# Attended values on 16 tiles of the TensorE array, turned by VectorE out of PSUM

## The reference, cut to what matters

```
attn = jax.nn.softmax(jnp.einsum('bthd,bshd->bhts', q, k) * scale, axis=-1)
attn_out = jnp.einsum('bhts,bshd->bthd', attn, v).reshape(Bc, Tc, INNER)
attn_out = attn_out @ out_w + out_b
x = x + gate1 * attn_out
```

## Time and profile before

| | |
|---|---|
| time, median of 3 runs | 338.66 us (338.62 to 338.73) |
| span of the profiled execution, first to last instruction | 336.9 us |
| busy: PE, DVE, ACT, POOL | 330.3, 215.2, 183.1, 121.5 us |
| chain that ended last | PE 88%, DVE 6%, ACT 4% |

### The profile page before, as it was taken

One profiled execution on the slowest core, in us unless ns is written; L12 is line 12 of the kernel. 1 busy time (PEld: TensorE's weight loads), 2 busy tenths in 40 slices (PEclk: granted clock), 3 DMA queues, 4 the chain that ended last, 5 costly groups with the idle time before them and its releaser, 6 DMA issues.

```text
span 336.9 us, 9816 instructions
## 1 busy us (share of the span) xinstructions
PE 330.3 (98%) x4197; PEld 299.6 (89%) x4197; DVE 215.2 (64%) x420; ACT 183.1 (54%) x356; POOL 121.5 (36%) x107
## 2 busy tenths in 40 slices
PE   8999999999999999999999999999999999999986
PEld 8989989899998989899898999889998889998765
DVE  3846966815858953505167236679565789886896
ACT  3754654454426365356423816478535576628794
POOL 1373405000934762555311413032620123304591
PEclk9999999999999999999999999999999999999999
DMA  7984930500045540110010000100010200200011
GB/s 241 369 283 175 299 129 2 151 8 2 2 146 170 158 158 34 64 33 2 3 56 11 2 20 14 43 24 2 2 62 2 64 3 2 64 2 2 0 33 62
DMA packets 20834, 24.41 MB, mean 72 GB/s; under 512 B 1780, under 2 KB 18328, under 8 KB 20792
## 3 DMA queue, kind: packets, MB, share of 16 engines
q1 hardware_dynamic: 20416, 23.50, 21.5%
q10 hardware_dynamic: 376, 0.30, 0.3%
HBM read 22.68 MB, written 1.11 MB: 71 GB/s over the span
## 4 chain that ended last, share of the span: by engine, by line
PE 88%; DVE 6%; ACT 4%; issue 1%; POOL 0%; DVEq 0%; ACTq 0%
PE proj_banks L564 40%; PE out_bank L564 15%; PE att_banks L657 8%; PE wide_banks L564 4%; PE turn_bank L564 3%; PE proj_banks L627 3%; PE wide_banks L848 2%; PE att_banks L564 2%; PE att_banks L892 1%; PE wide_banks L657 1%; ACT work L1855 1%; PE att_banks L848 1%; PE wide_banks L731 1%; ACT L1714 1%; DVE hamax L1466 1%
## 5 line engine op out<-in xcount | busy, mean ns | idle before, releaser
L1721 ACT ACTIVATE q_t<-proj_banks,bias_cols 128x256 f32<-128x256 f32 x64 | 30.6, 477 | 54.3 <-PE proj_banks L564 54.3
L564 PE MATMUL proj_banks<-x_hi,w_hi 128*128 128x256 f32 x252 | 52.8, 291 | 0.0
L564 PE MATMUL proj_banks<-x_lo,w_hi 128*128 128x256 f32 x252 | 50.7, 283 | 0.0
L564 PE MATMUL proj_banks<-x_hi,w_lo 128*128 128x256 f32 x252 | 50.7, 283 | 0.0
L1233 DVE TENSOR_TENSOR v_sb<-proj_banks,bv_row 128x512 f32<-128x512 f32 x32 | 21.7, 685 | 32.3 <-PE wide_banks L657 30.6
L564 PEld LDWEIGHTS proj_banks<-x_hi,w_hi 128*128 128x128 f32 x252 | 39.6, 191 | 1.5 <-issue 0.4
L564 PEld LDWEIGHTS proj_banks<-x_hi,w_lo 128*128 128x128 f32 x252 | 39.2, 191 | 0.0
L564 PEld LDWEIGHTS proj_banks<-x_lo,w_hi 128*128 128x128 f32 x252 | 39.2, 191 | 0.0
L657 PEld LDWEIGHTS att_banks<-probs_t,v_sb 32*128 32x128 f32 x512 | 29.8, 186 | 5.5 <-issue 5.4
L657 PE MATMUL att_banks<-probs_t,v_sb 32*128 32x32 f32 x512 | 31.6, 272 | 0.0
L1721 ACT ACTIVATE k_t<-proj_banks,bias_cols 128x256 f32<-128x256 f32 x64 | 30.2, 471 | 0.0
(11 more groups left out here) (324 smaller groups left out, 776.6 us busy)
## 6 DMA issues: line engine op xcount, KB each, us to landing
stage<-in_L_cond_qkv_w SPq DMA_DIRECT2D x16, 256.0 KB, 4.5
gate<-gate_rows_scratch SPq DMA_DIRECT2D x48, 64.0 KB, 2.4
stage<-in_L_cond_qkv_w SPq DMA_DIRECT2D x4, 512.0 KB, 5.0
stage<-in_L_cond_out_w SPq DMA_DIRECT2D x4, 512.0 KB, 4.3
work<-in_L_ffn_w SPq DMA_DIRECT2D x2, 1024.0 KB, 10.0
xin<-in_x SPq DMA_DIRECT2D x7, 256.0 KB, 2.9
bv_row<-in_L_cond_qkv_b SPq DMA_DIRECT2D x4, 256.0 KB, 5.7
work<-in_L_cond_ada_w SPq DMA_DIRECT2D x1, 1024.0 KB, 9.7
```

The lines of the kernel that those rows point to most:

```text
L564: mm = pe.matmul(dst, l, r, start=start and i == 0, stop=stop and i == len(seq) - 1)
L1721: act.activation(dst[:, h, :], proj_bank[h % 2][:, s * QT:(s + 1) * QT], ACT.Identity, bias=bias_cols[:, c:c + 1]).then_inc(qk_kept, 1)
```

## The change

In `attend` the operands change sides: the stationary operand is the 32x32 block of probabilities, the moving one the 32x128 block of values. The result is 32 tokens by 128 features, at the partitions of head h; with the sequence j as row tile and the head h as column tile all 16 tiles of 32x32 are used. A new `at_turn` on VectorE transposes the 32x32 blocks from PSUM into a new `at_raw` (in the memory of `at_lo`), two instructions of 128x512 elements per unit. `at_high` and `at_low` read `at_raw` in SBUF instead of PSUM, and work by tile t instead of by pair of banks. In the turned layout partition h*32+e holds feature d*32+e of head h, so the rows of the output weights are loaded in that order: four transfers for each group instead of one (128 KB each instead of 512 KB). PSUM is free again once `at_turned` is reached, so the waits for `at_lo_made` that guarded the banks become waits for `at_turned`. `out_proj` waits for its own t only, and for `at_lo` in both.

`attend(u - 1)` moves ahead: in units 1 to 7 before the last `qk_unit`, in the first units of the pairs from 8 on before the third, in the second units of the pairs before `v_unit(u, 0)`. In the second units of the pairs up to unit 13 `out_proj(u - 1, 0)` moves behind `ffn1` and the first `hq_turn`, and on VectorE `at_low` moves behind `softmax_shift`.

```diff
-    wo_d = out_w.rearrange("(h p) c -> p h c", p=P)
+    wo_d = out_w.rearrange("(g h d e) c -> g h e d c", g=NG, h=HG, d=HG)
...
+        at_raw = at("at_raw", [P, 2, HG, P], F32, floor.where["at_lo"])
...
         def att_from(u, p):
-            return att_pairs(u)[p][:, :, 0:2 * HG * TB].rearrange("p j (a c) -> p j a c", c=TB)
-
-        def att_to(split, p):
-            return split[:, :, :, 2 * p * TB:2 * (p + 1) * TB].rearrange("p t h (j c) -> p j (t h) c", j=2)
+            return att_pairs(u)[p][:, :, 0:2 * P].rearrange("p j (a c) -> p j a c", c=TB)
+
+        def att_to(p):
+            return at_raw[:, :, :, 2 * p * TB:2 * (p + 1) * TB].rearrange("p t d (j c) -> p j (t d) c", j=2)
...
             def load_wo(g):
-                sp.dma_start(wo_stage, wo_d[:, g * HG:(g + 1) * HG, :]).then_inc(wo_in, 16)
+                for h in range(HG):
+                    sp.dma_start(wo_stage[h * TB:(h + 1) * TB, :, :], wo_d[g, h]).then_inc(wo_in, 16)
...
                 if u > 0:
-                    pe.wait_ge(at_lo_made, 2 * u)
+                    pe.wait_ge(at_turned, 2 * u)
...
-                            dst = att_pairs(u)[j // 2][:, j % 2, (t * HG + h) * TB:(t * HG + h + 1) * TB]
-                            mm = pe.matmul(dst, v_sb[r, t, h * P:(h + 1) * P], probs_t[r, t * HG + h, :],
+                            dst = att_pairs(u)[j // 2][h * TB:(h + 1) * TB, j % 2, t * P:(t + 1) * P]
+                            mm = pe.matmul(dst, probs_t[r, t * HG + h, :], v_sb[r, t, h * P:(h + 1) * P],
                                            start=True, stop=True)
...
-                pe.wait_ge(at_hi_made, 2 * u + 2)
+                pe.wait_ge(at_hi_made, 2 * u + t + 1)
...
-                           late=("lhsT", (at_lo_made, 2 * u + 2)) if t == 0 else None).then_inc(out_mm, 1)
+                           late=("lhsT", (at_lo_made, 2 * u + t + 1))).then_inc(out_mm, 1)
...
-            def at_low(u, p):
-                dve.wait_ge(at_hi_made, 2 * u + p + 1)
-                dve.tensor_tensor(att_to(at_lo, p), att_from(u, p), att_to(at_hi, p).bitcast(F32),
-                                  ALU.subtract).then_inc(at_lo_made, 1)
+            def at_turn(u, p):
+                dve.wait_ge(attended, 2 * u + 2)
+                dve.transpose(att_to(p), att_from(u, p)).then_inc(at_turned, 1)
+
+            def at_low(u, t):
+                dve.wait_ge(at_hi_made, 2 * u + t + 1)
+                dve.tensor_tensor(at_lo[:, t], at_raw[:, t], at_hi[:, t].bitcast(F32), ALU.subtract).then_inc(at_lo_made, 1)
 
             def attention_tail(u):
                 if u > 0:
+                    for p in range(2):
+                        at_turn(u - 1, p)
                     keep_v(u, 0)
...
-            def at_high(u, p):
-                act.wait_ge(attended, 2 * u + 2)
-                act.copy(att_to(at_hi, p), att_from(u, p)).then_inc(at_hi_made, 1)
+            def at_high(u, t):
+                act.wait_ge(at_turned, 2 * u + 2)
+                act.copy(at_hi[:, t], at_raw[:, t]).then_inc(at_hi_made, 1)
```

73 lines of the change are left out of this document (43 added, 30 removed).

## The result

The changed kernel takes 344.17 us (median of 4, 342.68 to 345.94); the kernel before took 338.70 beside it. The ratio is 1.0165, interval 1.0131 to 1.0199. It is slower by 1.65%, where 0.4% faster was forecast (337.3, range 334.2 to 341.2). The profiled execution has a span of 342.7 us. The executions of the changed kernel spread by 1%, those of the kernel before by 0.1%.

A forecast was written before the change was run, and what follows sets the result against it. TensorE, busy 98% of the span, was taken to bound the kernel. Terms summed to a gain of 2.0, less 0.6 for `at_low` waits, about 1.4: span 336.9 to 335.5, with 1.8 around it 337.3 us, range 334.2 to 341.2.

The forecast's parts named there:

- The product: Attend on TensorE, each unit: 0.95 us instead of 1.92, saving 0.97 per unit, 15.5 us if nothing else waited.
- rivals 2 and 3: Middle attend: 1.38 us, 340.7, chance 0.12; attend not shorter, 1.8 to 1.9 us, column tiles taking turns: 344, chance 0.10.
- The turns: Two transposes on VectorE per unit, 0.71 us each: 1.34 with a little overlap, 21.5 us in all.
- less 0.6: Waits of `at_low` beside GpSimd: 0.6 us lost; bounds 0, and 2 us for each of two places on the path.
- The four transfers: Three more weight transfers per group: cost nothing while they land a unit early, their bytes being the same.
- Units 2, 4, 6: `score` or attend starts later behind VectorE's `x1_make`, `tern_keep`, `tern_make`, turns and `keep_v`: 0.6, 1.1 and 0.4 us lost.
- theory 2: Not in the prediction, tested after it: VectorE's instructions with two SBUF inputs wait for GpSimd's.
- Units 3, 5, 7, 8: Time gained: 0.7 us each in units 3, 5 and 7; 0.97 in unit 8, where VectorE is not behind.
- Unit 9: `at_low` comes behind the softmax's shift, `out_proj(8, 0)` waits 0.8 us for `at_lo`: only 0.14 gained.
- Units 12 to 15: VectorE's chain from `probs_t` nearly without a gap: 0.05 us gained in 12 and 13, 0.4 in 14 and 15.
- The tail: After unit 15, turns, `at_high` and `at_low` make `hidden_max` start 1.8 us later; with slack of 0.2, 1.6 lost.
- The rival on this side: Slower by VectorE: turns cost 0.89 us instead of 0.71, or `at_low` waits 2 in two places; 339 to 341, chance 0.18.

The follow-up runs named there:

- pieces: The changed kernel with GpSimd's subtractions on the weights each cut into four of a quarter of the size, nothing left out: 346.23 us, ratio 1.0225.
- one_wo: The changed kernel with one 512 KB transfer of output weights per group again, the order of the weights' rows left out: 343.34 us, ratio 1.0126.
- pool_after: The changed kernel with GpSimd's subtractions for the low parts of the weights replaced by fills with zero: 338.03 us, ratio 0.9986.

## Why the prediction was wrong, point by point

The forecast was 337.3, the time 344.17. Of the 6.9 us between them 4.1 are what `at_low` waited beside GpSimd beyond the 0.6 of the sum, up to 1.9 the four transfers, and about 1 the units 12 to 15.

- **The product.** 0.95 forecast, 0.99 measured, and on average a start every 12.6 ns. Right; so rivals 2 and 3 are out. That the time came to rival 3's 344 is chance: its mechanism isn't there. The Trainium skill's 25 ns between starts ("TensorE: Matmul & The Clock Gate", section "Wait — 56ns, not 53.3ns?") holds no more for 32x32 tiles with 128 columns than for `score`.
- **The turns.** 1.34 per unit forecast; 0.71 and 0.67 measured, less their overlap 1.31. Right.
- **`at_low` beside GpSimd, "less 0.6".** This is the step that failed: the term was 0.6, with 2 us for each of two places, 4 in all, as its upper bound, and it measured 4.7 (units 6 and 9 of pieces), or 6.1 with all that GpSimd's subtractions hold up. The three long `at_low` took 2.46 and 2.86 us in unit 8 and 2.88 in unit 5, and none took over 0.69 with GpSimd's reads gone. The row was there, 2266 ns at L1252, but "once" and "one case in 16" were misread from a minimum, a median and a maximum: four of these 16 took over 1 us in the kernel before, and their mean is 708 ns against a median of 426. I spread the wait as a chance over 32 instructions, when the trace of before shows which of them run beside one of GpSimd's subtractions of 128x1024: both `at_low(7)` beside `w_lo` (138.71 and 139.32, shown above), both `at_low(4)`, at 93.13 and 93.74, beside `f_lo`, and one of unit 8 at the end of a `wo_lo`. Three of these five are the long ones. The Trainium skill has the rule ("SBUF — State Buffer", section "SBUF: two separate sides"): the two engines shut each other out for a whole instruction. The trace agrees, with the 2.46 to 2.88 above. That the changed kernel without GpSimd's reads takes 338.03, near the 337.3 of the forecast, proves less than it seems: unit 2 also gains 1.84 there by weights that come earlier, and four of its ten executions have a stretch at clock 0.50.
- **The four transfers, "nothing while they land a unit early".** This failed too, as a term put at nothing. They are in time themselves; what stands behind them on SyncE is not. It is 0.5 us in unit 1 and 1.4 in unit 2 by one_wo's trace; the medians differ by 0.8. The sum asked only when these transfers land. It left out their issue, 1.4 us for the next transfer, and what they do to the landing of the weights behind them, 7.8 us instead of 5.8 (6.4 in one_wo).
- **Units 2, 4, 6.** In 2 and 4 the sign and the mechanism were right: score(2) waits 1.72 for `keep_v` behind the turns, attend(3) 0.69 for `tern_keep`. In pool_after, where theory 2 is absent, the pitches against before are +0.81, +1.59 and -0.33, forecast +0.6, +1.1 and +0.4 (here plus is time lost). So unit 6 gains without theory 2, and its loss was right in sign by luck: the 1.39 came from GpSimd.
- **Units 3, 5, 7, 8.** +0.7, +0.7, +0.7, +0.97 forecast; 0.72, 0.84, 0.43, 0.94 measured. Right, but for 0.3 in unit 7.
- **Unit 9.** +0.14 forecast, 1.96 lost; the wait of `out_proj(8, 0)` that I worked out as 0.8 is 0.44, and it stands behind score(9), so it counts in the next pitch. In pool_after the unit gains 0.96. The loss comes from unit 8.
- **Units 10, 11.** +0.97 and +0.1 forecast, 0.35 and 0.76 measured: the sum is right, the places are not.
- **Units 12 to 15.** +0.45 forecast, 0.8 lost, of which 0.4 (unit 12) is gone in pool_after. Here VectorE is late, and attend(12) and attend(14), now ahead of `v_unit`, wait 1.04 each for `probs_t`. The releaser isn't named, but the end of the transpose is at 228.31, and attend(12) starts at 228.41 (VectorE, then TensorE):

```profile
227.86 0.45 DVE L1263 STREAM_TRANSPOSE probs_t<-scores 128x256 f32<-128x256 f32 x1
```

```profile
228.41 0.30 PE L660 MATMUL att_banks<-v_sb,probs_t 32*32 32x128 f32 x2 [1.04 <-issue]
```

- **The tail.** 1.6 forecast, 61.2 - 59.6 = 1.6 measured. Right, and where it was said to be. VectorE in order of time, of the kernel before, to be held together with the earlier trace rows:

```profile
283.75 1.21 DVE L1463 TENSOR_TENSOR h_odd<-h_odd,g_row 128x1024 f32<-128x1024 f32 x1
...
286.30 1.21 DVE L1466 TENSOR_REDUCE hamax<-h_odd 128x1 f32<-128x1024 f32 x1
```

  And of the changed kernel:

```profile
288.59 1.21 DVE L1476 TENSOR_TENSOR h_odd<-h_odd,g_row 128x1024 f32<-128x1024 f32 x1
289.72 0.71 DVE L1267 STREAM_TRANSPOSE at_raw<-att_banks 128x512 f32<-128x512 f32 x1
290.36 0.67 DVE L1267 STREAM_TRANSPOSE at_raw<-proj_banks 128x512 f32<-128x512 f32 x1
291.71 1.29 DVE L1271 TENSOR_TENSOR at_lo<-at_raw,at_hi 128x512 fp32r<-128x512 f32 x2 [0.68 <-ACT at_hi L1750]
292.92 1.21 DVE L1479 TENSOR_REDUCE hamax<-h_odd 128x1 f32<-128x1024 f32 x1
```

  `hidden_max` starts 4.33 behind `hidden_weigh`; in the trace of before it is 286.30 - 283.75 = 2.55. That is 1.8 more, the number of the forecast.
- **The rival on this side** (4, 339 to 341) named the mechanism, with `at_low` waiting 2 us in two places; three `at_low` were up to 2.2 us too long, and the four transfers came on top. Its chance of 0.18 and its price were both too small, and only 0.6 of it stood in the forecast's sum.

## What to carry to other kernels

When an operand of a VectorE instruction moves from PSUM to SBUF, list which GpSimd instructions run beside it in the trace of before and in the new order, and add what is left of each; here that was up to 2.2 us. Cutting GpSimd's long instructions takes most of it away, at a price that matters only where something waits for them. A median hides such waits: read every instruction of the line. When a transfer is split, charge its issues to whatever is queued behind, and look at when the transfers behind it land. When a product gets shorter but its result needs a further step, find the latest place at which the work behind it still hides that step, not the earliest.

## What the runs showed of the hardware

- VectorE with two SBUF inputs (128x512) beside a GpSimd subtraction of 128x1024: 2.46 to 2.88 us instead of 0.69; beside one of a quarter of the size, at most 1.22. With one input in PSUM it stayed at 0.69 beside the same instruction in the kernel before. A cast with one SBUF input, `x_hi` L1153, waited as well (2.50 instead of 0.43).
- A moving operand of float32 with a stride of 4 elements makes the product 1.44 instead of 0.99 us (64 instructions of 128 columns on 16 tiles).
- A VectorE addition of 128x512 whose two inputs are read with a stride of 4 elements takes 1.07 instead of 0.68 us.
- Four transfers of 128 KB to 32 partitions each cost SyncE 0.34 to 0.43 us each to issue in unit 1; the first four, at 5.21, took 2.81 together. Four of the same size to 128 partitions each left the landing of the next weights as it was (median 6.0 us against 5.8); behind those to 32 partitions it was 7.8.
- A turn of 32x32 blocks on VectorE, 128x512 elements from PSUM, takes 0.67 to 0.71 us; 128x256 from SBUF takes 0.445.
- float32 instructions of 128 columns on the 16 tiles of 32x32 start on average every 12.6 ns (64 in 0.80 us).
